# Edge stage of a two-layer graph network on one core: relu layer and gate in two buffers each, and their products one group ahead of the core product

## The reference

```python
ei = concatenate([x[src], edge_attr], axis=-1)            # 256 + 64 columns
core = maximum(ei @ W1 + b1, 0.0) @ W2 + b2
gate = sigmoid(ei @ Wg + bg)
agg = segment_sum(gate * core, dst, num_segments=x.shape[0])
x = layernorm(x + (layernorm(agg + x) * gamma + beta))
# then: h = two hops of  segment_sum(h[row] * norm, col);  x = layernorm(x + log_softmax(h @ W.T + b))
```

## Time and profile before

| | |
|---|---|
| runs | 2704.09, 2691.65, 2703.35 us |
| median | 2703.35 us |
| profiled execution | span 2722.1 us; no time of its own besides the span is recorded for it |
| edge stage in the trace | about 146 to 1640 us |
| busy, share of the span | TensorE 88%, VectorE 76%, GpSimd 61%, ScalarE 55% |

### The profile page before, as it was taken

One profiled execution on the slowest core, in us unless ns is written; L12 is line 12 of the kernel. 1 busy time (PEld: TensorE's weight loads), 2 busy tenths in 40 slices (PEclk: granted clock), 3 DMA queues, 4 the chain that ended last, 5 costly groups with the idle time before them and its releaser, 6 DMA issues.

```text
span 2722.1 us, 50965 instructions
## 1 busy us (share of the span) xinstructions
PE 2389.6 (88%) x16049; PEld 1845.0 (68%) x16049; DVE 2076.2 (76%) x4860; ACT 1493.1 (55%) x2727; POOL 1663.0 (61%) x1581
## 2 busy tenths in 40 slices
PE   7879999999999999999899894689888899888864
PEld 3479999999999998888889881245444444444443
DVE  6658888888889888888889998897777763436455
ACT  1157777777767776676767674454665640112123
POOL 0367777777677776667667661456555645666663
PEclk9989999999999999999999996899999999998976
DMA  6555555555555555555555542254455425665542
GB/s 210 207 154 158 161 167 160 161 163 164 157 160 164 165 157 161 164 170 169 164 163 165 161 143 83 80 138 126 119 142 140 126 92 189 209 228 162 188 129 88
DMA packets 276289, 422.45 MB, mean 155 GB/s; under 512 B 127634, under 2 KB 198692, under 8 KB 274004
## 3 DMA queue, kind: packets, MB, share of 16 engines
q0 software_dynamic: 90368, 281.11, 34.6%
q1 hardware_dynamic: 170028, 116.99, 14.3%
q10 hardware_dynamic: 15656, 21.30, 2.3%
HBM read 354.91 MB, written 64.37 MB: 154 GB/s over the span
## 4 chain that ended last, share of the span: by engine, by line
PE 53%; DVE 18%; issue 9%; ACT 8%; another core or an unknown queue 7%; DMA 2%; DVEq 1%; POOL 1%; ACTq 1%; SPq 0%; POOLq 0%
PE banks L972 15%; PE banks L1060 5%; PE banks L949 5%; PE banks L1034 4%; PE banks L1086 3%; PE banks L856 3%; ACT counts L1432 2%; PE banks L1102 2%; PE banks L946 2%; DVE hidden_lo L1767 2%; PE banks L947 2%; ACT hidden_hi L1296 2%; DVE room L1786 2%; PE banks L960 2%
## 5 line engine op out<-in xcount | busy, mean ns | idle before, releaser
L797 POOL DMA_INDIRECT gathered<-p_table,src_t x784 | 807.2, 1030 | 439.7 <-DVE gate L1778 252.8
L797 POOL DMA_INDIRECT gathered<-hop_table,src_t x576 | 585.5, 1017 | 463.1 <-PE banks L1102 174.8
L972 PE MATMUL banks<-w_hi,hidden_hi 128*128 128x256 f32 x1568 | 462.1, 295 | 55.1 <-DVE hidden_lo L1767 48.6
L972 PE MATMUL banks<-w_lo,hidden_hi 128*128 128x256 f32 x1568 | 443.6, 283 | 0.0
L972 PE MATMUL banks<-w_hi,hidden_lo 128*128 128x256 f32 x1568 | 443.5, 283 | 0.0
L1432 ACT CAST counts<-banks 128x686 f32 (+3 forms) x382 | 295.4, 773 | 213.8 <-PE banks L1037 103.8
L1303 ACT CAST msg_hi<-room 128x512 fp32r<-128x512 f32 x392 | 241.8, 617 | 246.4 <-DVE room L1786 209.5
L1767 DVE SCALAR_TENSOR_TENSOR hidden_lo<-banks,hidden_hi 128x512 fp32r<-128x512 f32 x392 | 270.1, 690 | 121.8 <-ACT hidden_hi L1296 68.4
L972 PEld LDWEIGHTS banks<-w_hi,hidden_hi 128*128 128x128 f32 x1568 | 299.6, 191 | 79.0 <-DVE hidden_lo L1767 66.5
L1034 PE MATMUL banks<-codes,low_hot 128*128 128x343 f16 (+3 forms) x958 | 242.2, 337 | 111.2 <-DVE codes L2002 54.6
L1317 ACT ACTIVATE gate<-gate 128x512 f32<-128x512 f32 x392 | 242.3, 632 | 123.0 <-DVE gate L1778 107.1
(11 more groups left out here) (225 smaller groups left out, 5280.3 us busy)
## 6 DMA issues: line engine op xcount, KB each, us to landing
ea<-in_edge_attr SPq DMA_DIRECT2D x196, 128.0 KB
counts_saved<-counts SPq DMA_DIRECT2D x16, 1568.0 KB
ring<-counts_saved SPq DMA_DIRECT2D x16, 1568.0 KB
gathered<-p_table,src_t POOLq DMA_INDIRECT x784
p_table<-p_t ACTq DMA_DIRECT2D x48, 256.0 KB, 4.1
hop_table<-parts SPq DMA_DIRECT2D x12, 896.0 KB
gathered<-hop_table,src_t POOLq DMA_INDIRECT x576
x_saved<-x_room SPq DMA_DIRECT2D x7, 896.0 KB
```

The lines of the kernel that those rows point to most:

```text
L797: pool.indirect_dma_start(out=rows[:, n % slots, j, :], out_offset=None, in_=table[:, :], in_offset=bass.IndirectOffsetOnAxis(ap=src_t[:, ...
L972: last = nc.tensor.matmul(banks[:, 4 + half, j % 2 * H:(j % 2 + 1) * H], lhs, rhs, start=False, stop=n == len(products) - 1, skip_group_ch ...
```

## The change

TensorE makes the hidden and gate products of group g+1 ahead of the core product of group g in the same step. For this `gate`, `hidden_hi` and `hidden_lo` get two buffers each, and `ea_turned_sb` goes down to one. `copy_ea` then waits for the gate product of the group before, and `upper_hidden` and `add_gate` wait one group less far back. ScalarE's and VectorE's steps get new orders. GpSimd's `lower_msg` runs four groups behind the gather in place of three. The bias of the core product is kept once and read twice by `seed_core`, and each half of it follows the `upper_msg` of the same half. Some small tables move in SBUF.

```diff
+MSG_LAG = 4
...
-        ea_turned_sb = at("ea_turned_sb", EDGE_AT + 14336, [P, 2, GROUP], F32R)
-        gate = at("gate", EDGE_AT + 18432, [P, TILES, H])
-        hidden_hi = at("hidden_hi", 75264, [P, KC, GROUP], F32R)
-        hidden_lo = at("hidden_lo", 79360, [P, KC, GROUP], F32R)
+        bias_core = at("bias_core", EDGE_AT + 8192, [P, H])
+        ea_turned_sb = at("ea_turned_sb", EDGE_AT + 9216, [P, GROUP], F32R)
+        gate = [at(f"gate{n}", EDGE_AT + 11264 + 4096 * n, [P, TILES, H]) for n in range(2)]
+        hidden_lo = [at(f"hidden_lo{n}", where, [P, KC, GROUP], F32R) for n, where in enumerate((79360, EDGE_AT + 19456))]
+        hidden_hi = [at(f"hidden_hi{n}", where, [P, KC, GROUP], F32R) for n, where in enumerate((75264, 107136))]
...
             for g in range(NG):
-                if g >= 3:
-                    lower_msg(g - 3)
+                if g >= MSG_LAG:
+                    lower_msg(g - MSG_LAG)
                 gather(p_table, gathered, 2, 0, "p_gathered", "gate_added", 2, g)
...
                 def step(i, s):                      # TensorE
-                    at_group(core_product, i, s, 0)
                     at_group(hidden_product, i, s, 1)
                     at_group(gate_product, i, s, 1)
+                    at_group(core_product, i, s, 0)
                     at_group(scatter_stage, i, s, -1)
                     at_group(turn_ea, i, s, 3)
...
             def copy_ea(turn, s, g):                 # ScalarE
                 act.wait_ge(S["ea_turned"], g + 1)
-                wait_count(act, S["gate_product"], 2 * (g - 1))
-                nc.scalar.copy(ea_turned_sb[:, s, :], banks[:, 7, :]).then_inc(S["ea_ready"], 1)
+                wait_count(act, S["gate_product"], 2 * g)
+                nc.scalar.copy(ea_turned_sb[:, :], banks[:, 7, :]).then_inc(S["ea_ready"], 1)
...
                     if k == 0:                       # upper_hidden
-                        wait_count(act, S["core_done"], 2 * g)
+                        wait_count(act, S["core_done"], 2 * (g - 1))
...
-            def seed_core(turn, s, g):
-                for half in range(2):
+            def seed_core(half):
+                def stage(turn, s, g):
                     wait_count(act, S["msg_ready"], 2 * g + half - 1)
-                    nc.scalar.copy(banks[:, 4 + half, :], bias_core[:, :, :].rearrange("p j n -> p (j n)")).then_inc(
-                        S["core_seeded"], 1)
+                    nc.scalar.copy(banks[:, 4 + half, :].rearrange("p (j n) -> p j n", j=2),
+                                   bias_core.unsqueeze(1).to_broadcast([P, 2, H])).then_inc(S["core_seeded"], 1)
+                return stage
...
             def step(i, s, in_order=True):           # ScalarE
+                at_group(upper_hidden(0), i, s, 1)
+                at_group(upper_hidden(1), i, s, 1)
                 at_group(copy_ea, i, s, 2)
+                at_group(open_gate, i, s, 1)
                 at_group(round_ea, i, s, 4)
                 if in_order and isinstance(i, int):
                     node_rows_at(2 * i + s)
-                at_group(upper_msg(0), i, s, 0)
-                at_group(upper_hidden(0), i, s, 1)
-                at_group(upper_msg(1), i, s, 0)
-                at_group(upper_hidden(1), i, s, 1)
-                at_group(seed_core, i, s, 1)
-                at_group(open_gate, i, s, 1)
+                for half in range(2):
+                    at_group(upper_msg(half), i, s, 0)
+                    at_group(seed_core(half), i, s, 1)
...
             def add_gate(turn, s, g):                # VectorE
-                wait_count(dve, S["msg_ready"], 2 * g)
+                wait_count(dve, S["msg_ready"], 2 * (g - 1))
...
                 at_group(add_window, i, s, -2)       # step_in_order, VectorE
                 at_group(lower_msg, i, s, -1)
                 node_work_at(0)
+                at_group(lower_hidden(0), i, s, 1)
+                node_work_at(1)
+                at_group(lower_hidden(1), i, s, 1)
+                node_work_at(2)
+                at_group(add_gate, i, s, 1)
+                node_work_at(3)
                 at_group(lower_ea, i, s, 4)
-                node_work_at(1)
+                at_group(one_hot, i, s, 0)
+                node_work_at(4)
                 at_group(message, i, s, 0)
-                at_group(one_hot, i, s, 0)
-                node_work_at(2)
-                at_group(lower_hidden(0), i, s, 1)
-                at_group(lower_hidden(1), i, s, 1)
-                node_work_at(3)
-                at_group(add_gate, i, s, 1)
-                node_work_at(4)
                 node_work_at(5)
```

More of the change, by code:

```diff
@@ L957, in gate_product @@
                     for j in range(2 * half, 2 * half + 2):
-                        to, lhs = banks[:, 2 + half, j % 2 * H:(j % 2 + 1) * H], ea_turned_sb[:, s, j * P:(j + 1) * P]
+                        to, lhs = banks[:, 2 + half, j % 2 * H:(j % 2 + 1) * H], ea_turned_sb[:, j * P:(j + 1) * P]
                         nc.tensor.matmul(to, lhs, w_e_hi[:, H:H2], start=True, stop=False)
@@ L968, in core_product @@
                     for j in range(2 * half, 2 * half + 2):
-                        products = [(a[:, k, j * P:(j + 1) * P], b[:, k, :]) for k in range(KC)
+                        products = [(a[s][:, k, j * P:(j + 1) * P], b[:, k, :]) for k in range(KC)
                                     for a, b in ((hidden_hi, w_2_hi), (hidden_hi, w_2_lo), (hidden_lo, w_2_hi))]
@@ L1253, in _ @@
             load(w_l[:, :, :], Wl.rearrange("(k p) n -> p k n", p=P), "setup_loaded")
-            for half in range(2):
-                load(bias_core[:, half, :], b2.partition_broadcast(P), "setup_loaded")
+            load(bias_core, b2.partition_broadcast(P), "setup_loaded")
             for to, of in ((gamma_all, gamma), (beta_all, beta)):
@@ L1315, in open_gate @@
                     act.wait_ge(S["gate_added"], 2 * g + half + 1)
-                    rows = gate[:, 2 * half:2 * half + 2, :]
+                    rows = gate[s][:, 2 * half:2 * half + 2, :]
                     nc.scalar.activation(rows, rows, ACT.Sigmoid).then_inc(S["gate_ready"], 1)
@@ L1777, in add_gate @@
                     tiles = slice(2 * half, 2 * half + 2)
-                    nc.vector.tensor_tensor(gate[:, tiles, :], banks[:, 2 + half, :].rearrange("p (j n) -> p j n", j=2),
+                    nc.vector.tensor_tensor(gate[s][:, tiles, :], banks[:, 2 + half, :].rearrange("p (j n) -> p j n", j=2),
                                             gathered[:, s, tiles, H:H2], ALU.add).then_inc(S["gate_added"], 1)
@@ L1786, in message @@
                     nc.vector.tensor_tensor(msg_of(msg, s, half), banks[:, 4 + half, :].rearrange("p (j n) -> p j n", j=2),
-                                            gate[:, 2 * half:2 * half + 2, :], ALU.mult).then_inc(S["msg_ready"], 1)
+                                            gate[s][:, 2 * half:2 * half + 2, :], ALU.mult).then_inc(S["msg_ready"], 1)
             def lower_msg(turn, s, g):
@@ L1839, in step_anywhere @@
                 at_group(lower_msg, i, s, -1)
-                at_group(lower_ea, i, s, 4)
-                at_group(message, i, s, 0)
                 at_group(lower_hidden(0), i, s, 1)
@@ L1844, in step_anywhere @@
                 at_group(add_gate, i, s, 1)
+                at_group(lower_ea, i, s, 4)
+                at_group(message, i, s, 0)
             def worked(c, q):
```

35 lines of the change are left out of this document (17 added, 18 removed).

## The result

The changed kernel takes 2880.61 us (median of 4 runs, 2877.51 to 2881.88) against 2703.72 (2691.65 to 2706.45): 1.0673 of before, 95% interval 1.0654 to 1.0691, or 177 us more. The forecast was 2798, with 2747 to 2849 as its range. The direction is right, and the time lies 32 us outside the range.

The account below looks back on a forecast made before the run. TensorE was taken as the bound, waiting 0.3 to some 0.8 us per group. The new VectorE–ScalarE turn plus half the node pieces added 34.5, 23.6, 26.7 and 10.6, together 95 us, to 2703.35: 2798 us, range 2747 to 2849.

Parts of the forecast that it names:

- The ring: Edge stage: VectorE and ScalarE wait for each other in a closed turn, 7.80 us per group without node pieces.
- The wait at `lower_ea`: VectorE waits for ScalarE's `round_ea`, now behind `open_gate`: 1.01 us of the turn, about 0.9 idle.
- The seed in two halves: ScalarE's `seed_core` reads the bias twice and keeps its duration, pair 1.11 us.
- the size of the node pieces on the ring: VectorE's node pieces: half lengthen the turn, 0.28, 0.47 and 0.55 us per group in the later stretches.
- places 0 and 5: Slots for node pieces between VectorE's `message` and next `lower_hidden(0)`: covered by a wait, so free.
- 2.0 us of cover: VectorE's time between the end of `message` and next `lower_hidden(0)`: hides `add_window` and `lower_msg`, 1.4 us, at no cost.
- The rival of GpSimd's `lower_msg`: It holds VectorE's pieces between the two `lower_hidden`: 0.15 us per group, about 18 us, 2816 us; chance 0.2.
- all of the pieces on the ring: Upper bound: every VectorE node piece lengthens the turn, +146 us in place of +95.
- The open ring: One link missing, TensorE's 7.04 us per group decides early: down to 2606 us, more likely near 2640; chance 0.08.
- The balance: VectorE's instructions overlap more, a turn of 7.4 us per group: 2690 to 2716 us; chance 0.04.
- What stayed hidden: Single `ea_turned_sb`, gathers, GpSimd's lag of four and setup: cost nothing in the edge stage.

Follow-up runs that it names:

- e1: Changed kernel with ScalarE's `round_ea` of g+4 moved ahead of `open_gate` of g+1: 2741.39 us, 1.0074 of before.
- e2: Changed kernel with VectorE's `lower_ea` of g+4 moved behind the message of g, ScalarE's order kept: 2749.59 us, 1.0073 of before.
- e3: Changed kernel with the seed of half 1 moved behind the next group's `upper_hidden`: 2851.61 us, 1.0459 of before.
- e8: Changed kernel with GpSimd's `lower_msg` subtraction replaced by a memset that reads nothing, leaving out that low part: 2830.29 us, 1.0374 of before.
- e10: Changed kernel with the edits of e5 and e8 together: 2803.86 us, 1.0278 of before.
- e5: Changed kernel with node pieces only at the three of six places where VectorE waits for ScalarE: 2824.08 us, 1.0356 of before.
- e6: Changed kernel with the edits of e1 and e5 together: 2700.08 us, 0.9899 of before.
- e13: Kernel before, in its own order, with the edit of e5 alone: 2741.24 us, 1.0045 of before.
- e12: The kernel of e6 measured once more: 2700.79 us, 0.9897 of before.
- e9: The kernel of e6 with all six places again for the last chunk, groups 186 to 195: 2700.84 us, 0.9899 of before.
- e4: Changed kernel with the edits of e1 and e3 together: 2805.64 us, 1.0286 of before.

## Why the prediction was right in direction and wrong in size

**The ring holds.** Measured 7.85 per group against 7.80. The 0.05 comes from ScalarE's four instructions, which follow each other at 0.52 us (2.09 together) where the four of before took 2.01. The wait at `lower_ea` is 0.99 against a forecast 1.01 of distance with "about 0.9" idle. The seed in two halves kept its price. Over 78 groups this term was off by 4 us. By e1 and e2 the link at `lower_ea` is real and opens from either end; by e3 the seeds are on it too.

**The step that failed is the size of the node pieces on the ring**: "I put half of it on the ring, three of six places", with places 0 and 5 taken as free and GpSimd's hold left to a rival. In us per group, averages over steps worked out from the starts in the traces:

| part of the ring | after, 4–78 | after, 112–132 | e8, 112–132 |
|---|---|---|---|
| `lower_hidden(0)` to the end of `add_gate` (places 1, 2) | 2.48 | 2.97 | 2.72 |
| to `lower_ea` (3) | 0.99 | 0.99 | 0.99 |
| to `message` (4) | 0.94 | 1.06 | 1.06 |
| `message` to `upper_hidden(0)` | 2.80 | 2.87 | 2.88 |
| to `lower_hidden(0)` (5, 0) | 0.62 | 0.91 | 0.63 |

Without GpSimd's reads (e8) the pieces cost 0.24 at places 1 and 2 and 0.12 at place 4, the last part stays at 0.63, and the whole is 0.44 above the early steps, near the 0.47 of the forecast. With the reads there come 0.25 at places 1 and 2 and 0.28 ahead of `lower_hidden(0)`, together 0.53.

Half of the pieces was thus right for the pieces alone, but that the sum agrees so well is in part luck. The forecast halved 0.94 us, read from VectorE's busy time in before, which held instructions had already lengthened (28 us over groups 78 to 195, next table). In e8 VectorE is busy 6.55 us per group from 110 to 168, so the bare pieces are 0.72 (less 5.83, the early 6.22 with `add_window` halved); half of that is the 0.36 of the table. The missing 0.08 is no piece but ScalarE's `upper_rows`, which stands once per chunk ahead of `upper_hidden(0)` (once in the 20 steps of either column) and which the forecast had left out (count; shortest, median and longest ns):

```profile
L1371 ACT ACTIVATE parts<-agg x7: 1694/1697/1703, 1148.8 to 1838.0; 128x1792 f16<-128x1792 f32 x7
```

The hold costs as much again, and half of it falls where the prediction had 2.0 us of cover: pieces of places 5 and 0 and VectorE's `lower_msg` fill that room with `add_window`, and when one of them is held, `lower_hidden(0)` starts late. The pieces themselves bring this about. On average GpSimd's `lower_msg` starts 0.50 us behind `lower_hidden(0)` in the early groups and 0.37 us ahead of it in groups 110 to 168, since the pieces push `lower_hidden(0)` back. VectorE's `lower_msg` is held in none of the 74 early steps, and in 7 of those 58.

The traces can also be counted. Held is here an instruction of VectorE that overlaps GpSimd's `lower_msg` and lasts over 0.25 us longer than the same instruction mostly does without it; groups 78 to 195.

| | before | after | e8 | e10 | e1 | e5 | e6 | e13 |
|---|---|---|---|---|---|---|---|---|
| held instructions | 36 | 68 | 4 | 0 | 60 | 17 | 18 | 52 |
| time added, us | 28 | 66 | 1 | 0 | 56 | 23 | 21 | 46 |

The account in the trace, measured less forecast: 0.05 x 78 + 0.27 x 32 + 0.61 x 58 + 0.71 x 27 = 3.9 + 8.6 + 35.4 + 19.2 = 67 us, and 95 + 67 = 162 of the 165.5 measured. Of the 63 behind group 78, the difference between after and e8 gives 0.27 x 32 + 0.56 x 58 + 0.68 x 27 = 59. So the hold is nearly the whole miss in the edge stage, and the 66 us that are counted in the changed kernel agree with it. The median missed by 83 us: 70 are in the edge stage, another 20 of the medians' difference lie between runs and profiles, as said above, and 8 came back outside the edge stage. Why the runs of before beside the result (2703 us) were so much shorter than its profiled execution (2722) stays open; on the three chips of the experiments before took 2726 to 2729.

**The rival of GpSimd's `lower_msg`** had the mechanism and the direction, but at one place of six and 0.15 us per group; it is 0.27 in groups 78 to 110 and about 0.6 behind. The upper end of the range had the same fault: "all of the pieces on the ring" counts each at its own duration, and a held piece costs up to ten times that. The rule of the Trainium skill (page "SBUF — State Buffer", section "Who interferes with whom") should have been applied to every instruction of VectorE with two inputs in SBUF that stands near `lower_msg` on the new ring, not to one place. The trace agrees: in e8, where GpSimd only writes the same tile and reads nothing, the two kinds of piece shown last 0.165 and 0.482 us at the longest. The page also says that a GpSimd instruction which only writes does not contend with such two-input instructions; e8 bears that out. Two inputs are not the whole of it: 13 of the 68 held instructions of the changed kernel are `TENSOR_SCALAR` with one.

**The open ring** (2606 to 2640) is not what the change does, but e1 and e6 are that case, and it was priced too well. 7.04 was one step of TensorE; where TensorE is busiest with the ring open, a step takes 7.14 to 7.25 (e1 up to group 78, e6 up to 110). The rows had it: TensorE's busy time of the first stretch is 529.51/74 = 7.16 us per group. And VectorE's later groups did not fall to its busy time: e1 has 7.94 and 8.22 there, above before. At its best (e6, e12, e9) the new order gains 29 to 31 us of edge stage in the trace.

**The balance** at 7.4 is refuted by the 7.85 of the early groups.

**What stayed hidden, as forecast**: the single `ea_turned_sb` (of TensorE's waits in the edge stage of after 0.8 us in all are put down to it; in e1 ScalarE waits 72 us in 61 steps before `copy_ea`, by the code for the gate product, beside a TensorE that is busy 99%), the gathers, the lag of four, the setup. TensorE's granted clock stayed at 0.97 to 0.99 too.

**Open.** e13 is slower than before by 11 us of edge stage; it has 18 us more of held time, which fits, but no run takes that away. In e6 21 us of held time are left, 13 of them in the last stretch; how much of this is on its path would need e8's edit as well. The long wait of e4 is open too.

## What to carry to other kernels

Before buffers are added to let one engine run ahead, follow one turn of the other engines' written orders through every semaphore: a wait for an item that its producer has behind the result of the waiting engine closes a ring, here 7.85 us where the engine that was to be freed needs 7.2. Move the producer up (one line, e1) before anything else. Small pieces of side work belong where the host engine waits anyway, and are priced at what they last beside a neighbour that holds them, not at their own duration.

## What was not expected of the hardware

GpSimd's two-input instruction of 1.2 us in SBUF stretched VectorE instructions of 0.16 us to 1.56, of 0.47 to 1.82 and of 0.69 to 2.39. Over the later groups this is about 0.6 us of 8.9 per group. A GpSimd write of the same tile that reads nothing (e8) held none of the 58 two-input instructions that it overlapped (one, started within a held piece, took 0.14 us more), but it held four short `TENSOR_SCALAR` pieces with one input in SBUF, 0.16 us otherwise, to 0.46 to 0.62; beside the subtraction such pieces lasted up to 1.56. Instructions that take one input from PSUM and one from SBUF were not held by either: `lower_hidden` lasts at most 0.69 us with or without GpSimd beside it.

Two things about it were not expected. The VectorE instruction need not start second: the piece at 1314.38 started 0.31 us ahead of GpSimd's at 1314.69 and ended behind it all the same, and the `lower_msg` at 1323.15 started 0.63 us ahead of GpSimd's at 1323.78, nearly its own length of 0.69. And that one lasted 2.39 us, more than both together (0.69 + 1.20). No run here explains either; the start that the trace gives may not be the moment at which an instruction takes its operands.
